# Linear attention on one core: values, keys and queries turned through DRAM and VectorE in place of TensorE

## The reference

```python
mixed = silu(causal_conv4(hidden @ W_qkv));  q, k, v = split(mixed)
z = hidden @ W_z;  beta = sigmoid(hidden @ W_b)
g = -exp(A_log) * softplus(hidden @ W_a + dt_bias)
q = l2norm(q) * DK ** -0.5;  k = l2norm(k)          # each key head serves 2 value heads
for t in tokens:                                     # a state S (128 x 128) per value head
    S = S * exp(g[t])
    v_adj = (v[t] - k[t] @ S) * beta[t]
    S = S + outer(k[t], v_adj)
    o[t] = q[t] @ S
attn = (rmsnorm(o) * norm_weight * silu(z)) @ W_out
ffn = sum over the 2 chosen experts: softmax weight * (gelu(x @ w1 + b1) @ w2 + b2)
out = x + attn * silu(ffn)
```

## Time and profile before

| | us |
|---|---|
| median of three runs | 2076.37 |
| lowest, highest | 2072.62, 2080.99 |
| the profiled execution's own time | 2080.1 |
| span of the profiled execution | 2078.3 |
| mean granted TensorE clock | 0.985 |

### The profile page before, as it was taken

One profiled execution on the slowest core, in us unless ns is written; L12 is line 12 of the kernel. 1 busy time (PEld: TensorE's weight loads), 2 busy tenths in 40 slices (PEclk: granted clock), 3 DMA queues, 4 the chain that ended last, 5 costly groups with the idle time before them and its releaser, 6 DMA issues.

```text
span 2078.3 us, 39559 instructions
## 1 busy us (share of the span) xinstructions
PE 2008.6 (97%) x13730; PEld 1713.5 (82%) x13730; DVE 1353.6 (65%) x3169; ACT 909.1 (44%) x2525; POOL 834.1 (40%) x2123
## 2 busy tenths in 40 slices
PE   5789999999999999999999999999999999999999
PEld 3578888888888888888888888888888888887887
DVE  6868877778688878787777445555555444446442
ACT  4555555555465555556555532222223232233221
POOL 1456666666575766666565511100010210101111
PEclk9889999999999999999999999999999999999999
DMA  4233545343535444434443232443334434303441
GB/s 125 51 74 79 97 84 100 79 96 80 89 84 94 92 97 81 97 81 97 88 87 71 77 93 59 94 92 81 77 76 92 118 86 99 69 26 122 152 143 70
DMA packets 388022, 184.25 MB, mean 89 GB/s; under 512 B 249456, under 2 KB 369136, under 8 KB 385776
## 3 DMA queue, kind: packets, MB, share of 16 engines
q1 hardware_dynamic: 354640, 177.73, 37.8%
q10 hardware_dynamic: 33184, 4.01, 1.3%
HBM read 135.26 MB, written 46.40 MB: 87 GB/s over the span
## 4 chain that ended last, share of the span: by engine, by line
PE 69%; issue 10%; DVE 6%; DMA 5%; POOL 4%; ACT 3%; SPq 2%; ACTq 0%; POOLq 0%; DVEq 0%
PE bank L333 17%; PE bank L335 17%; PE bank L334 17%; DMA VT<-v_dram 4%; PE bank L565 3%; PE bank L574 2%; PE bank L548 2%; PE bank L468 2%; PE bank L584 2%; PE bank L556 2%; PE bank L527 2%; PE bank L533 1%; POOL y_out L1823 1%; POOL V L1771 1%; POOL prod L1769 1%
## 5 line engine op out<-in xcount | busy, mean ns | idle before, releaser
L1769 POOL TENSOR_TENSOR prod<-A_in,V 128x60 f32<-128x60 f32 (+24 forms) x992 | 301.4, 304 | 269.6 <-DMA A_in<-a_dram 199.3
L1771 POOL TENSOR_TENSOR V<-V,prod 128x60 f32<-128x60 f32 (+24 forms) x992 | 311.1, 314 | 77.8
L1098 ACT ACTIVATE hid<-bank,bias 128x512 f32<-128x512 f32 x128 | 88.3, 690 | 455.3 <-PE bank L335 453.5
L1813 POOL TENSOR_TENSOR ffn_w_lo<-ffn_raw,ffn_w_hi 128x1024 fp32r<-128x1024 f32 x32 | 77.9, 2437 | 470.3 <-ACT ffn_w_hi L1088 466.4
L1563 DVE TENSOR_TENSOR h_lo<-hid,h_hi 128x512 fp32r<-128x512 f32 x128 | 91.1, 712 | 265.8 <-ACT h_hi L1105 265.8
L1577 DVE SCALAR_TENSOR_TENSOR gate_acc<-bank,rw,gate_acc 128x512 f32<-128x512 f32 x240 | 177.6, 748 | 58.8 <-PE bank L335 58.8
L333 PE MATMUL bank<-ffn_w_hi,h_hi 128*128 128x512 f32 x512 | 199.3, 389 | 1.2 <-DVE h_lo L1563 1.0
L333 PE MATMUL bank<-xn_hi,ffn_w_hi 128*128 128x512 f32 x512 | 200.3, 391 | 0.0
L335 PE MATMUL bank<-xn_hi,ffn_w_lo 128*128 128x512 f32 x512 | 199.2, 389 | 0.0
L334 PE MATMUL bank<-xn_lo,ffn_w_hi 128*128 128x512 f32 x512 | 199.2, 389 | 0.0
L335 PE MATMUL bank<-ffn_w_hi,h_lo 128*128 128x512 f32 x512 | 199.2, 389 | 0.0
(11 more groups left out here) (224 smaller groups left out, 5178.0 us busy)
## 6 DMA issues: line engine op xcount, KB each, us to landing
E<-eg_dram SPq DMA_DIRECT2D x64, 256.0 KB, 8.1
A_in<-a_dram SPq DMA_DIRECT2D x32, 512.0 KB, 4.0
decb<-dec_dram SPq DMA_DIRECT2D x128, 128.0 KB, 4.2
og_dram<-og SPq DMA_DIRECT2D x64, 256.0 KB, 2.2
ffn_raw<-w SPq DMA_DIRECT2D x32, 512.0 KB, 4.0
og_x<-og_dram SPq DMA_DIRECT2D x256, 64.0 KB, 2.7
ogT_dram<-og_y SPq DMA_DIRECT2D x64, 256.0 KB, 2.4
og_in<-ogT_dram SPq DMA_DIRECT2D x16, 1024.0 KB, 5.2
```

Source lines behind the costliest of these rows:

```text
L1098: act.activation(hid[:, i % 2, :], bank[i % 4][:, :], ACT.Gelu_apprx_tanh, bias=bias1[:, k, f * NF + ft:f * NF + ft + 1]).then_inc(S_["gel ...
L1769: pool.tensor_tensor(prod[:, 0:m, 0:n], column, V[:, vb, 0:m, j:j + 1].to_broadcast([P, m, n]), MUL).then_inc(S_["product"], 1)
L1771: pool.tensor_tensor(V[:, vb, 0:m, j + 1:B32], V[:, vb, 0:m, j + 1:B32], prod[:, 0:m, 0:n], ADD).then_inc(S_["solve_step"], 1)
L1813: pool.tensor_tensor(fw[m, "lo", n % 2][:, :], raw[:, i % 2, :], fw[m, "hi", n % 2][:, :].bitcast(f32), SUB).then_inc(S_["ffn_lo"], 1)
```

## The change

The sixteen TensorE transposes of a block are gone. In their place:

- `load_kq(b)`: SyncE stores keys and queries of a block (`kqT`, one tile of 128 x 1024 floats) to `kq_dram`, waits until this has landed, and issues four loads into `kq_x`. Each load fills 32 partitions with 32 rows of 32 floats (128 bytes): groups of 32 of one side are exchanged with groups of 32 of the other. It stands at the end of a step, behind the store of `og`.
- `load_v(b)`: the same for the two value heads, behind the fourth `next_decay` of the next step.
- `turn_kq(b)` on VectorE: two 32x32-block transposes of 128x512, keys into `k_rem`, then queries in place; behind `convolve(st + 1, "k")`, ahead of `chain_R` of chunk 2. `turn_v(b)`: two more, into `v_tok`, behind `chain_S` of chunk 3, ahead of `convolve(st, "v0")`.
- ScalarE's squares, `put_k` and `put_v` now read SBUF and work in place. `squares_q` moves from the head of a step to its third quarter, one step later; both `put_v` move to the end of a step, around `put_y64`.
- Some tiles lose a buffer (`v_tok`, `og`), and waits change with the banks and tiles they guarded.
- "Coefficient in two operations": `neg_inv` = -(1 + exp(-b)) is kept, so that c_neg is one product and one reciprocal (two small operations where there were four per half block); `key_remains` does the remaining factor and the added epsilon once a block.

Cut to its core:

```diff
+        vs_dram = nc.dram_tensor("vs_dram", (B32, NQD, REP * SB), f32, kind="Internal").ap()
+        kq_dram = nc.dram_tensor("kq_dram", (B32, NQD, 2 * SB), f32, kind="Internal").ap()
...
-        v_tok = alloc(p2b, "v_tok", [2, CPS, REP * HD])
-        og = alloc(p2b, "og", [2, 2, REP, HD])
+        kq_x = alloc(p2b, "kq_x", [NQD * 2 * CPS, B32])
+        v_x = alloc(p2b, "v_x", [NQD * REP * CPS, B32])
+        og = alloc(p2b, "og", [2, REP, HD])
+        v_tok = alloc(p2b, "v_tok", [REP, CPS, HD])
...
+        X_SET = 16 + 16 * NQD
...
 def attention_step(st):                       # tensor
                 if chain:
                     chain_keys(st - 2, 0)
-                if now:
-                    turn_q(st)
                 if chain:
                     join_z64(st - 2)
...
-                if turned:
-                    turn_v(st, 0)
                 if chain:
                     chain_keys(st - 2, 2)
...
-                if turned:
-                    turn_v(st, 1)
-                    turn_k(st)
                 if chain:
                     chain_keys(st - 2, 3)
...
 def attention_step(st):                       # scalar
-                if now:
-                    squares_q(st)
...
-                if turned:
-                    put_v(st, 0)
...
                 if turned:
-                    put_v(st, 1)
+                    squares_q(st - 1)
                     put_k(st)
...
                 if turned:
+                    put_v(st, 0)
                     put_y64(st - 1)
+                    put_v(st, 1)
...
-                dve.tensor_scalar(norms[:, bb, r2], norms[:, bb, r2], L2_EPS, None, ADD).then_inc(S_["nk_eps"], 1)
-                dve.wait_ge(S_["nk_eps"], n)
-                dve.reciprocal(inv_n[:, r2], norms[:, bb, r2]).then_inc(S_["inv_n"], 1)
-                dve.wait_ge(S_["inv_n"], n)
-                dve.tensor_tensor(c_neg[:, bb, r2, :], neg_beta[:, cg, h0:h0 + REP],
-                                  inv_n[:, r2].rearrange("p (c o) -> p c o", o=1).to_broadcast([P, 2, REP]), MUL).then_inc(S_["c_neg"], 1)
+                dve.scalar_tensor_tensor(c_neg[:, bb, r2, :], norms[:, bb, r2].rearrange("p (c o) -> p c o", o=1).to_broadcast([P, 2, REP]), L2_EPS,
+                                         neg_inv[:, cg, h0:h0 + REP], ADD, MUL).then_inc(S_["nk_beta"], 1)
+                dve.wait_ge(S_["nk_beta"], n)
+                dve.reciprocal(c_neg[:, bb, r2, :], c_neg[:, bb, r2, :]).then_inc(S_["c_neg"], 1)
                 dve.wait_ge(S_["c_neg"], n)
-                dve.tensor_tensor(c_rem[:, bb, r2, :], c_neg[:, bb, r2, :], remain[:, cg, h0:h0 + REP], MUL).then_inc(S_["c_rem"], 1)
...
+            def turn_kq(b):
+                dve.wait_ge(S_["kq_x"], X_SET * (b + 1))
+                if b >= 2:
+                    dve.wait_ge(S_["state_add"], CPS * (b - 1))
+                elif b:
+                    dve.wait_ge(S_["rows_out"], 32 * NSB)
+                kq = kq_x[:, :, :].rearrange("p (b c a) j -> p a c b j", b=NQD, a=2)
+                dve.transpose(k_rem[b % 2][:, :, 0, :].rearrange("p c (b j) -> p c b j", b=NQD), kq[:, 0, :, :, :]).then_inc(S_["k_turned"], 1)
+                dve.wait_ge(S_["k_turned"], b + 1)
+                dve.transpose(kq[:, 0, :, :, :], kq[:, 1, :, :, :]).then_inc(S_["q_turned"], 1)
+
+            def turn_v(b):
+                dve.wait_ge(S_["v_x"], X_SET * (b + 1))
+                if b:
+                    dve.wait_ge(S_["R"], CPS * b)
+                for h in range(REP):
+                    src = v_x[:, :, :].rearrange("p (b m) j -> p m b j", b=NQD)[:, h * CPS:(h + 1) * CPS, :, :]
+                    r = dve.transpose(v_tok[:, h, :, :].rearrange("p c (b j) -> p c b j", b=NQD), src)
+                r.then_inc(S_["v_turned"], 1)
...
 def attention_step(st):                       # vector
-                if now:
-                    query_norms(st)
                 if ahead:
                     convolve(st + 1, "k")
+                if turned:
+                    turn_kq(st - 1)
                 if chain:
                     chain_R(st - 2, 2)
...
                 if chain:
                     chain_S(st - 2, 3)
+                if turned:
+                    query_norms(st - 1)
+                    turn_v(st - 1)
                 if now:
                     convolve(st, "v0")
...
+            def load_v(b):
+                sp.wait_ge(S_["act_v0"], b + 1)
+                sp.wait_ge(S_["act_v1"], b + 1)
+                if b:
+                    sp.wait_ge(S_["v_turned"], b)
+                else:
+                    sp.wait_ge(S_["xT"], 14)
+                sp.dma_start(vs_dram.rearrange("i b t -> b i t"), vS[:, :, :].rearrange("p h t -> p (h t)")).then_inc(S_["v_x"], 16)
+                sp.wait_ge(S_["v_x"], X_SET * b + 16)
+                for q in range(NQD):
+                    r = slice(q * B32, (q + 1) * B32)
+                    src = vs_dram.rearrange("i b (m t) -> i (b m) t", t=P)[:, :, r]
+                    sp.dma_start(v_x[r, :, :], src).then_inc(S_["v_x"], 16)
...
 def attention_step(st):                       # sync
                 next_decay(2)
                 next_decay(3)
+                if turned:
+                    load_v(st - 1)
...
                 if chain:
                     store(2 * (st - 2))
+                if now:
+                    load_kq(st)
...
             load_blocks(1)
+            load_v(0)
+            load_kq(1)
             sp.wait_ge(S_["rows_out"], 96)
             load_growth(2, 0)
```

More of the change, by code:

```diff
@@ L459, in pair_matrices @@
                 pe.wait_ge(S_["act_q"], b + 1)
[L460 to L463, removed]
+                if half == 0 and is_block(st):
+                    pe.wait_ge(S_["CP"], CPS * (st + 1))
                 elif half == 1:
@@ L469, in pair_matrices @@
                 r.then_inc(S_["pair_kq"], 1)
[L471 to L503, removed]
             def join_y32(b):
@@ L510, in join_y32 @@
                     at = slice(ch * B32, (ch + 1) * B32)
[L511 to L512 removed]
+                    pe.matmul(bank[LA][32:64, at], Cn(b, ch)[0:32, 32:64], VY64[0:32, ch, 0:32], start=True, stop=True)
+                    r = pe.matmul(bank[LB][96:128, at], Cn(b, ch)[64:96, 96:128], Y32[64:96, ch, :], start=True, stop=True)
                 r.then_inc(S_["lev_y32"], 1)
@@ L526, in join_y64 @@
                 for ch in range(NCH):
-                    r = pe.matmul(bank[LA][64:128, ch * 64:(ch + 1) * 64], Cn(b, ch)[0:64, 64:128], V64[0:64, ch, :], start=True, stop=True)
+                    r = pe.matmul(bank[LA][64:128, ch * 64:(ch + 1) * 64], Cn(b, ch)[0:64, 64:128], VY64[0:64, ch, :], start=True, stop=True)
                 r.then_inc(S_["lev_y64"], 1)
@@ L532, in join_z64 @@
                 for ch in range(NCH):
-                    r = pe.matmul(bank[LB][0:64, ch * 64:(ch + 1) * 64], Y64[64:128, ch, :], VT[64:128, b % 2, ch, 64:128], start=True, stop=True)
+                    r = pe.matmul(bank[LB][0:64, ch * 64:(ch + 1) * 64], VY64[64:128, ch, :], VT[64:128, b % 2, ch, 64:128], start=True, stop=True)
                 r.then_inc(S_["lev_z64"], 1)
@@ L573, in chain_state @@
                 for h in range(REP):
-                    r = pe.matmul(bank[K_BANK][:, h * HD:(h + 1) * HD], k_rem[:, b % 2, i, h, :], U[:, n % 2, h, :], start=True, stop=True)
+                    r = pe.matmul(bank[K_BANK][:, h * HD:(h + 1) * HD], k_rem[b % 2][:, i, h, :], U[:, n % 2, h, :], start=True, stop=True)
                 r.then_inc(S_["state_add"], 1)
@@ L740, in tensor @@
             turn_x(10)
-            turn_q(0)
             pair_matrices(-1, 0)
@@ L757, in tensor @@
             turn_x(15)
-            turn_q(1)
             pair_matrices(0, 0)
@@ L767, in tensor @@
             project_z(1, 1)
-            turn_v(1, 0)
             project_q(1)
             project_z(1, 2)
-            turn_v(1, 1)
-            turn_k(1)
             project_v0(1)
@@ L888, in silu @@
                     if b:
-                        act.wait_ge(S_["v_turned"], 2 * b)
+                        act.wait_ge(S_["v_x"], X_SET * b)
                     dst = vS[:, int(kind[1]), :]
@@ L910, in put_k @@
                 act.wait_ge(S_["k_turned"], b + 1)
-                act.wait_ge(S_["c_rem"], 2 * b + 2)
-                if b >= 2:
-                    act.wait_ge(S_["state_add"], CPS * (b - 1))
+                act.wait_ge(S_["c_rem"], b + 1)
                 for c in range(CPS):
-                    for h in range(REP):
-                        i = act.mul(k_rem[:, b % 2, c, h, :], TK_BANK[:, c * P:(c + 1) * P], c_rem[:, b % 4, c, h:h + 1])
+                    for h in (1, 0):
+                        i = act.mul(k_rem[b % 2][:, c, h, :], k_rem[b % 2][:, c, 0, :], c_rem[:, b % 4, c, h:h + 1])
                 i.then_inc(S_["k_rem"], 1)
@@ L920, in put_v @@
                 b = st - 1
-                act.wait_ge(S_["v_turned"], 2 * b + half + 1)
+                act.wait_ge(S_["v_turned"], b + 1)
```

(13 more changed lines are left out.)

130 lines of the change are left out of this document (72 added, 58 removed).

## The result

The changed kernel takes 2401.92 us (2400.57 to 2404.59, 4 runs) where the kernel before takes 2076.34 (2072.62 to 2080.99): a ratio of 1.157, 95% interval 1.155 to 1.159. It is slower by 326 us, four times the 82 that were forecast, and outside the range.

What follows compares the result with a forecast made beforehand. The prediction took the chain's dependency loop, not TensorE's 97% load, as the bound where it waits for chain_S. Sum: 2080 + 0 + 62 + 16 + 3 = 2161, so a median of 2158 us; range 2066 to 2235.

Steps and rivals of the forecast that it cites:

- (f): Values' DRAM round trip at the step's end: store 1.8, loads 5.6, values 2.2 us late; 62 us in all.
- (h): Keys' and queries' DRAM round trip at the step's end, a whole step to hide it: 0; prologue trips 3 us.
- (a): First half of the value transposes, second quarter: they fill time TensorE waits for chain_S anyway; removal worth 0.
- (d): `turn_kq` ahead of chain_R of chunk 2 makes TensorE's product wait: mean loss 0.57 us a step.
- (b): Second half of the value transposes and the key transposes, ahead of third-quarter `chain_keys`: removal worth 0.44 us a step.
- (c): Query transposes directly ahead of `join_z64`: of their 0.53 us about 0.1 left as gain, `put_y64` standing behind `put_v`.
- (e): Coefficient in fewer small VectorE operations, some 0.4 us less ahead of chunk 0's chain_S: worth 0, cost 0.
- (g): TensorE's clock at 0.50 after waits for late values, counted in ten steps: 16 us (ends 0 and 52).
- much slower: Rival: 128-byte DMA rows at the upper end, clock drop each step: 2300, likelier 2190 to 2240 us; chance 0.20.
- No change: Rival: values land in time, store 1.0 and loads 4.3 us: 2076 to 2086 us; chance 0.17.
- faster: Rival: values in time and chain_R of chunk 2 not late, transposes' gain holds in full: 2046 us; chance 0.12.

## Why the prediction was wrong

**The direction and the path were right.** The values' round trip is on the loop; they come late at `turn_v`, and from there the wait runs over `put_v` and `put_y64` to `join_z64`, as (f) has it.

**The store in (f) was mis-sized, and that is the step that failed.** It was taken as 1.8 us behind decb's landing, with ends of 1.0 and 4.0, from the 512 KB load of the earlier trace rows and the words "few and long rows". It measured 4.8 us behind the landing in the step shown (4.9 in the median), and the keys' store 10.4 us by itself. The row it was sized by is a load with 128 pieces counted outermost; the bytes were the same, the number of engines was not. The upper end of 4.0 was no bound, since nothing in the trace before had a transfer of the store's shape. The other terms of (f) stand: on 16 engines the store took 1.3 (in the median too), the loads 6.1 in the step shown (6.7 in the median) against 5.6, and the values were 2.2 us late in that step, 1.9 in the mean, against the 2.2 predicted.

**(h) put the keys' and queries' trip at 0; alone it cost 121 us**, the place of `turn_kq` and the coefficient's small gain included. The working gave it "some 6 us where the queue otherwise sits still for about 7". With the store at 9.6 us instead of some 2 that doesn't fit, and SyncE's wait for it holds up what is queued behind. Cut in four, the trip costs nothing, and with only the wait moved it costs some 20 us: so (h)'s judgement was right for the store that it assumed, and wrong by the same mis-sizing. The prologue was put at 3 us (0 to 14) and cost 23, 18.0 of them in one wait of `chain_keys` for the S that `zero_state` clears, which the change moved from ahead of the steps into the first one, behind VectorE's late work; without the trips the prologue still cost 9, with 5.3 in that wait. The prediction didn't price that move.

**(a) to (d): zero in sum was too kind.** No run tests (a) by itself. (d) is right: the solve of chunk 2 stood still 0.46 to 0.49 us a step against 0.57. But of the 0.44 us of (b) and the 0.1 of (c) little or nothing arrived: with `turn_q` and `turn_k` alone gone a step is at best 0.13 us shorter, and with all transposes gone and no transfer it is 0.67 longer. The prediction looked at one `chain_keys` at a time and held the rest of the loop fixed. Its 6.2 us for sixteen transposes, set beside the 1.8 of the rows, rest on the figure of the Trainium skill ("VectorE: DVE Perf Modes", The three transpose paths) for one bf16 transpose; these are fp32 and overlap, and nothing in the sum hangs on it.

**(e)** at 0: some 6 us in fact, within what it called no difference.

**(g)** at 16 us (ends 0 and 52): filling the wait gave back 11 us (some 20 by the estimate above). The clock fell 37 times in the steps, not in ten of them, and 372 us at half clock are far more than ten times 3.3; each drop cost much less than its length.

**Of the rivals**, much slower had the right kind and too small an end: it took the store at 4.0 and the loads at 7.0 us and came to 2300. No change and faster had the chances of a store that takes all engines; even then the time is 2191.

What stays open: with both stores cut and `turn_kq` moved, the kernel (2191.13) is 123 us above the one that keeps the values on TensorE (2068.26). `join_z64`'s wait is 85 of them and the prologue 11. The remaining 27 or so were not taken apart.

## What to carry to other kernels

Before a DMA is sized by another of the same bytes, look at what both sides count outermost: a view that puts 4 in front uses 4 engines, and splitting both stores by hand into transfers with 32 in front cost a few more issues and gave back 211 us. A wait on an in-order queue is priced by what stands behind it, not by the transfer itself: with the same slow store, the kernel was 121 us slower with the wait directly behind it and about 20 with the wait moved, 16 of them TensorE's wait for the R that `turn_kq` holds up. And taking filler off an engine at 97% is worth only what the dependency loop beneath it leaves: here 0.98 us of transposes a step were worth 0.13 at most.

## What the runs showed of the hardware

- A store of 512 KB in 32 by 4 pieces of 4096 bytes ran at an engine share of 0.24 to 0.27 and took 10.4 us alone. With both stores cut in four of 32 pieces, each store of keys and queries lands 2.7 us after its issue in the median, each of the values, issued behind decb, 4.0 (the DMA issues of that kernel's page):

```profile
kq_dram<-kqT SPq DMA_DIRECT2D x128, 128.0 KB, 2.7
kq_x<-kq_dram SPq DMA_DIRECT2D x128, 128.0 KB, 3.8
...
vs_dram<-vS SPq DMA_DIRECT2D x128, 128.0 KB, 4.0
```

- Four loads of 1024 pieces of 128 bytes went at a share of 0.91 with 155 GB/s, two loads of weights beside them, and took 6.2 us against 5.6 predicted: short pieces are not what the prediction missed. Cheap they are not: such a piece took 14 ns of an engine, 9 GB/s, one of 4096 bytes in the values' store 159 ns, 26 GB/s.
- A mean clock that is higher by 0.035 was worth 11 us of 2400, by the estimate above up to some 20, while the steps were bound by transfers: here the low clock behind a wait was a sign of the wait, and only in small part a cost of its own.
